# Down projection as a 2x2 block product with seven products, in a fused four-layer kernel on one Trainium2 core

## The reference

```python
gate = lora_add(einsum('bnh,fh->bnf', x, W_gate), x, A_gate, B_gate)
up   = lora_add(einsum('bnh,fh->bnf', x, W_up), x, A_up, B_up)
act  = silu(gate) * up                                   # F = 2752 features
down = lora_add(einsum('bnf,hf->bnh', act, W_down), act, A_down, B_down)   # H = 1024
x = x + down
```

## Time and profile before

| engine | busy us | share of the span | instructions |
|---|---|---|---|
| PE | 1717.8 | 96% | 8904 |
| PEld | 1472.5 | 82% | 8904 |
| DVE | 1136.5 | 63% | 1713 |
| ACT | 686.6 | 38% | 1095 |
| POOL | 341.7 | 19% | 407 |

### The profile page before, as it was taken

How to read it: one execution, slowest core, us unless ns; L and a number is a source line. 1 busy time by engine, 2 the same in 40 slices (tenths; PEclk the granted TensorE clock), 3 DMA queues, 4 the chain that set the end, 5 groups by cost and what they waited for, 6 DMA issues and landing times.

```text
span 1797.5 us, 28151 instructions
## 1 busy us (share of the span) xinstructions
PE 1717.8 (96%) x8904; PEld 1472.5 (82%) x8904; DVE 1136.5 (63%) x1713; ACT 686.6 (38%) x1095; POOL 341.7 (19%) x407
## 2 busy tenths in 40 slices
PE   6889999999998999998999999999989899989998
PEld 6778888888887887887888888888877777879997
DVE  4866667667754654335766666666658744348887
ACT  4333333333333442322333333333324322236655
POOL 5332222222220000001222222222210004002330
PEclk9899999999999999998999999999989999999999
DMA  8553323323334665534333233233235534466654
GB/s 253 186 137 106 103 93 105 105 94 108 107 118 152 210 215 192 189 135 160 101 104 102 95 106 103 93 104 106 76 111 187 175 109 153 158 242 236 241 181 188
DMA packets 100879, 258.00 MB, mean 144 GB/s; under 512 B 14818, under 2 KB 19074, under 8 KB 99810
## 3 DMA queue, kind: packets, MB, share of 16 engines
q1 hardware_dynamic: 73010, 186.70, 31.0%
q0 software_dynamic: 15728, 48.74, 8.7%
q10 hardware_dynamic: 12096, 22.03, 3.3%
HBM read 214.13 MB, written 49.58 MB: 147 GB/s over the span
## 4 chain that ended last, share of the span: by engine, by line
PE 80%; DVE 7%; issue 4%; SPq 3%; DMA 3%; ACT 2%; POOLq 1%; POOL 0%; another core or an unknown queue 0%; DVEq 0%; ACTq 0%
PE ps L1065 63%; PE ps L1319 5%; PE ps L1103 4%; PE ps L1316 3%; SPq L429 1%; DVE whl L1751 1%; DMA wraw<-in_wd 1%; PE ps L1348 1%; PE ps L1142 1%; PE ps L1144 1%; PE ps L1076 1%; ACT whl L736 1%; SPq L426 1%; PE ps L1332 1%; DVE act_hl L1755 1%
## 5 line engine op out<-in xcount | busy, mean ns | idle before, releaser
L1065 PE MATMUL ps<-act_hl,whl 128*128 128x512 f32 x2016 | 468.2, 394 | 14.2 <-DVE act_hl L1755 10.8
L1065 PE MATMUL ps<-xop,aop_a 128*128 128x512 f32 x2016 | 472.7, 390 | 0.0
L1065 PEld LDWEIGHTS ps<-act_hl,whl 128*128 128x128 f32 x2016 | 380.9, 190 | 99.7 <-DVE act_hl L1755 15.5
L1065 PEld LDWEIGHTS ps<-xop,aop_a 128*128 128x128 f32 x2016 | 372.9, 188 | 73.9
L1065 PE MATMUL ps<-xop,aop_b 128*128 128x512 f32 x1512 | 367.4, 392 | 6.7 <-DVE t L1714 6.3
L1065 PEld LDWEIGHTS ps<-xop,aop_b 128*128 128x128 f32 x1512 | 279.6, 189 | 62.2 <-DVE t L1714 4.9
L1751 DVE TENSOR_TENSOR whl<-wraw,whl 128x1024 fp32r<-128x1024 f32 x96 | 121.3, 1264 | 248.2 <-ACT whl L736 233.5
L736 ACT ACTIVATE whl<-wraw 128x1024 fp32r<-128x1024 f32 (+2 forms) x132 | 115.1, 888 | 355.9 <-PE ps L1065 297.3
L578 POOL DMA_INDIRECT lb_raw<-in_bgu,row_b x168 | 172.2, 1025 | 81.5 <-issue 38.4
L592 POOL TENSOR_SCALAR row_b<-row_b 128x4 int32<-128x4 int32 x40 | 24.0, 601 | 628.1 <-DVE lb_hl L1702 628.0
L1685 DVE TENSOR_TENSOR aop_b<-raw,aop_b 128x512 fp32r<-128x512 f32 x84 | 58.1, 692 | 107.8 <-ACT aop_b L736 107.7
(11 more groups left out here) (226 smaller groups left out, 2127.5 us busy)
## 6 DMA issues: line engine op xcount, KB each, us to landing
wraw<-in_wd SPq DMA_DIRECT2D x88, 512.0 KB
raw<-in_wgu SPq DMA_DIRECT2D x168, 256.0 KB, 3.1
rtoep<-k_dram SPq DMA_DIRECT2D x64, 512.0 KB, 4.3
act_raw<-act_dram SPq DMA_DIRECT2D x84, 256.0 KB
act_dram<-t ACTq DMA_DIRECT2D x42, 256.0 KB, 2.0
act_dram<-u ACTq DMA_DIRECT2D x42, 256.0 KB
xn<-in_x SPq DMA_DIRECT2D x16, 512.0 KB, 8.0
x0r<-x_dram POOLq DMA_DIRECT2D x16, 512.0 KB, 5.4
```

Of the source, the lines that this page charges most:

```text
L1065: ins = pe.matmul(bank, wt, r, start=start and k == 0 and n == 0, stop=stop and k == nk - 1 and n == 2, skip_group_check=True)
```

## The change

**The block product.** The first 20 feature tiles are two halves of ten (`NK = 10`), the 1024 outputs two halves of four banks. Halves of features, of outputs and the two chunks give a 2x2 block product, done with the same seven products as gate/up. Each product runs over ten tile pairs k. The 21st tile and the rest of 64 features (a "tail" step), and the LoRA product (an "adapt" step), are added as before, once for each of the four blocks of the result.

```diff
+def down_steps():
+    def tail(seg, block):
+        return [(seg, "tail", block, 0), (seg, "adapt", block, 0)]
+    def tiles(seg, i, ks):
+        return [(seg, "product", i, k) for k in ks]
+    return (tiles(0, Q1, range(NK)) + tiles(1, Q6, range(NK)) + tiles(2, Q2, range(NK)) + tail(2, (0, 0))
+            + tiles(3, Q5, range(NK)) + tiles(4, Q7, range(NK)) + tiles(6, Q3, range(NK // 2))
+            + tail(5, (1, 1)) + tiles(6, Q3, range(NK // 2, NK)) + tail(6, (0, 1))
+            + tiles(7, Q4, range(NK)) + tail(7, (1, 0)))
+GROUP = (0, 1, 0, 1, 0, 0, 1, 0)
+BANKS = ((6, 7, 0, 1), (2, 3, 4, 5))
+DIFFS = [i for i, d in enumerate(DOWN) if d[1] == "product" and d[2] in (Q6, Q7, Q4)]
+RAW_RING, HL_RING = 4, 3
```

```diff
+            def difference(p, s):
+                dve.wait_ge(draw_in[r], 32 * (total * p + m))
+                dve.wait_ge(y_in[n % 2], 16 * (len(DIFFS) // 2 * p + n // 2 + 1))
+                b = draw[r][:, 1, :]
+                tt(b, b, ysub[n % 2][:, :], ALU.subtract).then_inc(diff_done, 1)
...
+            def down(p, after):
+                for s in range(2, ND):
+                    if s + 1 in DIFFS:
+                        difference(p, s + 1)
+                    down_lo(p, s)
+                    for piece in after.get(s, ()):
+                        piece()
```

**In the frames.** DVE makes the other difference operand (activations of chunk 1 minus chunk 0) and it is stored too. In pass 0, frames 1 to 20 also make the four sums of weights that the products need, from a 512 KB load by SP, and POOL stores them (512 KB) to DRAM for both passes:

```diff
+            def weight_sums(v):
+                a11, a21, a12, a22, s1 = (wsum[:, i, :] for i in range(5))
+                dve.wait_ge(ws_in, 16 * (v + 1))
+                tt(s1, a21, a22, ALU.add).then_inc(ws_sum, 1)
+                dve.wait_ge(ws_sum, 4 * v + 1)
+                tt(a22, s1, a11, ALU.subtract).then_inc(ws_sum, 1)
+                tt(a21, a11, a21, ALU.subtract).then_inc(ws_sum, 1)
+                dve.wait_ge(ws_sum, 4 * v + 2)
+                tt(a12, a12, a22, ALU.subtract).then_inc(ws_sum, 1)
@@ DVE frame, after a_low of Q7 and Q2 and before the add of g1
+                if p == 0 and not (isinstance(f, int) and f == 0):
+                    weight_sums(f - 1)
@@ DVE frame, before the last act_low
+                if not last:
+                    tt(g0[:, :], t5[:, :], u3[:, :], ALU.subtract).then_inc(d_made, 1)
@@ POOL
             for f in range(1, NF):
                 load_lb(0, f)
+                pool.wait_ge(ws_sum, 4 * f)
+                pool.dma_start(ws_dram[f - 1], wsum[:, 1:5, :]).then_inc(ws_stored, 16)
@@ SP, end of the loads of frame f in pass 0
+                    reach(sp, ws_stored, 16 * (f - 1))
+                    sp.dma_start(wsum[:, 0:4, :].rearrange("p a w -> p (a w)"), wds[f - 1]).then_inc(ws_in, 16)
```

More of the change, by code:

```diff
@@ L432, in down_loads @@
[L432 to L464, removed]
@@ new lines, in down_loads @@
+            def down_loads(p):
+                for s in range(ND):
+                    load_down(p, s)
+                    if p and s == 50:
+                        sp.wait_ge(d_ev, n_evd(1, 4, 1))
+                        for i in range(4):
+                            sp.wait_ge(x1_stored[i], 16)
+                        sp.dma_start(x1s[:, 1, :, :], x1_dram[1]).then_inc(x1_in, 16)
+                if p:
+                    sp.wait_ge(k_stored, 32)
+                    sp.dma_start(x1s[:, 0, :, :], x1_dram[0]).then_inc(x1_in, 16)
@@ L790, in xraw_free @@
                 else:
-                    eng.wait_ge(x1_stored, 16 * 2)
+                    for i in range(4):
+                        eng.wait_ge(x1_stored[i], 16)
             def a_split(p, f, i):
@@ new lines, in frame, with down_hi @@
+                act_split(p, f, 1, 6, last)
+                act_split(p, f, 0, 8, last)
+                if not last:
+                    act.wait_ge(d_made, n_st(p, f) + 1)
+                    act.dma_start(act_dram[p, 2, f], g0[:, :]).then_inc(d_stored, 16)
+            def down_hi(p, s):
+                r = s % RAW_RING
+                kind = DOWN[s][1]
+                if kind == "adapt":
+                    act.wait_ge(bd_in, 32 * (4 * p + ADAPT.index(s) + 1))
+                else:
+                    n = sum(q % RAW_RING == r and q not in ADAPT for q in range(s + 1))
+                    total = sum(q % RAW_RING == r and q not in ADAPT for q in range(ND))
+                    act.wait_ge(draw_in[r], 32 * (total * p + n))
+                if s in DIFFS:
+                    act.wait_ge(diff_done, len(DIFFS) * p + DIFFS.index(s) + 1)
+                if s == 0:
+                    act.wait_ge(prod, n_f(p, NF - 1, PER_F) + USED_AT[Q7])
+                elif s == 1:
+                    act.wait_ge(prod, n_f(p, NF - 1, PER_F) + USED_AT[Q6])
+                elif s == 2:
+                    act.wait_ge(act_lo, n_act(p, NF))
+                else:
+                    act.wait_ge(*step_done(p, s - HL_RING))
+                copy(dhl[s % HL_RING][:, 0, :, :], draw[r][:, :, :]).then_inc(d_hi, 1)
@@ new lines, in save_p1, with form_last @@
+            def save_p1(p):
+                for half in range(2):
+                    act.wait_ge(d_done, bank_done(p, 0, 2 * half + 1))
+                    copy(p1_sb[p][:, 2 * half:2 * half + 2, :], banks_of(0, half)).then_inc(p1_saved, 1)
+            def down(p, after):
+                for s in range(2, ND):
+                    down_hi(p, s)
+                    for piece in after.get(s, ()):
+                        piece()
+            def form_last():
+                act.wait_ge(d_ev, n_evd(0, 4, 1))
+                form_hi(1, 6)
@@ new lines, in down_step @@
+            def down_step(p, s):
+                seg, kind, what, _ = DOWN[s]
+                hl = dhl[s % HL_RING]
+                begins = s == FIRST[seg]
+                start = begins and seg not in (2, 5, 6)
+                pe.wait_ge(d_lo, n_lo(p, s))
+                if kind == "adapt":
+                    pe.wait_ge(t_ready, p * 10 + 9 + what[1])
+                for j, b in enumerate(BANKS[GROUP[seg]]):
+                    if begins:
+                        free_banks(p, seg, j)
+                    cols = slice(j * P, j * P + P)
+                    bank = ps[:, b, :]
+                    if kind == "product":
+                        ins = split3(bank, lambda _: hl[:, 0, 0, cols], lambda _: hl[:, 1, 0, cols],
+                                     lambda _: hl[:, 0, 1, :], lambda _: hl[:, 1, 1, :], 1, start)
+                    elif kind == "tail":
+                        c = what[1]
+                        split3(bank, lambda _: hl[:, 0, 0, cols], lambda _: hl[:, 1, 0, cols],
+                               lambda _: act_hl[:, c, 0, :], lambda _: act_hl[:, c, 1, :], 1, False)
+                        for i in range(2):
+                            ins = pe.matmul(bank, hl[:, i, 1, cols], act_rest[:, c, :], start=False, stop=False,
+                                            skip_group_check=True)
+                    else:
+                        c = what[1]
+                        for half in range(2):
+                            for i in range(2):
+                                ins = pe.matmul(bank[:, half * HT:half * HT + HT], hl[:, i, half, cols],
+                                                t_hl[:, c, 0, half, :], start=False, stop=half == 1 and i == 1,
+                                                skip_group_check=True)
+                    if s == FINAL[seg]:
+                        ins.then_inc(d_done, 1)
+                if s != FINAL[seg]:
+                    ins.then_inc(d_used, 1)
@@ L1256, in _, with down @@
+            def down(p):
+                for s in range(ND):
+                    if p and s == 2:
+                        a_down(1, NF - 1)
+                    if p and s == FINAL[5] + 4:
+                        pe.wait_ge(d_ev, n_evd(1, 7, 1))
+                        s4d_kernel()
+                    down_step(p, s)
             for q in range(NQ):
@@ L1550, in kernel_rows @@
                 dve.wait_ge(kp, 1)
-                did(dve.tensor_copy(ksb[:, :, :].rearrange("p h j -> p (h j)"),
-                                    ps[0:LS, 0:4, :].rearrange("p a b -> p (a b)")))
+                for half in range(2):
+                    did(dve.tensor_copy(
+                        ksb[:, half * (C // 2):(half + 1) * (C // 2), :].rearrange("p (a h) j -> p a (h j)", a=2),
+                        banks_of(0, half)[0:LS, :, :]))
                 after()
@@ new lines, in difference @@
+            def difference(p, s):
+                n = DIFFS.index(s)
+                r = s % RAW_RING
+                m = sum(q % RAW_RING == r and q not in ADAPT for q in range(s + 1))
+                total = sum(q % RAW_RING == r and q not in ADAPT for q in range(ND))
+                dve.wait_ge(draw_in[r], 32 * (total * p + m))
+                dve.wait_ge(y_in[n % 2], 16 * (len(DIFFS) // 2 * p + n // 2 + 1))
+                b = draw[r][:, 1, :]
+                tt(b, b, ysub[n % 2][:, :], ALU.subtract).then_inc(diff_done, 1)
@@ L1832, in pass_, with down @@
+            def down(p, after):
+                for s in range(2, ND):
```

(10 more changed lines are left out.)

658 lines of the change are left out of this document (332 added, 326 removed).

## The result

The changed kernel took 1782.12 us in the median of four runs (1780.02 to 1782.82), the kernel before 1797.32 (1795.31 to 1799.87): a ratio of 0.9913, 95% interval 0.9896 to 0.993. That is 15 us faster where 68 were forecast: 37 us above the forecast's 1712 to 1745, and 14 us above the wider range that ends at 1768. The profiled execution spans 1780.7 us, 16.8 less than before.

What follows compares the result with a forecast made beforehand. PE was taken to bound the frames and pass 0's down stage, with DVE limiting part of pass 1's. Terms of -54.7, 0, -10, -4, -4, -7, +5 and +7 sum to -67.7 us: 1730 us forecast, range 1712 to 1745.

Steps and rivals of the forecast that it cites:

- Fewer matmuls: Tile steps: 240 fewer matmuls of 512 columns at 0.2278 us, -54.7 us if PE stays the bound.
- Splitting: Pass 0's down stage: DVE's splitting keeps up and PE stays the bound, 0 us, between -3 and +10.
- State-space kernel: Pass 1's down stage: losses of 20.4 us shrink to 10, so -10 us, between -17 and 0.
- The seams: Waits around the down stages shrink: pass 0's seam -4, between the passes -4, pass 1's restart -7 us.
- Frames of pass 0: Gathers behind the store of sums make a 22.2 us loop: +5 us over 20 frames, bounds 0 and +34.
- the sign that the prediction had set itself: The prediction is wrong if pass 0's frames are above 22.6 us.
- Rival B: Pass 0's frames: POOL's gather lands late, loop 23.7 us, +34 in place of +5, 1759 us; chance 0.12.
- Loads of the difference steps: Down stages: tiles for difference steps sometimes land late, +7 us, bounds 0 and +58.
- rival C: Down stages: difference-step loads land in 10 us, +94 in place of +7, 1817 us; chance 0.09.
- A: Only the matmuls go: no loss shrinks, frames cost 5 and steps 7 us, 1755 us; chance 0.17.
- A's 15: Sign for A: PE waits over 15 us on DVE's splits in steps 2 to 26 of pass 1.

Runs made afterwards that it cites:

- e5: e2 with pass 1's eight 512 KB residual loads moved from steps 6 to 9 to steps 24 to 27 of the down stage: 1723.7 us.
- e10: e2 plus the edits of e5 and e8, with the 2 MB x1 load cut into four at steps 50, 54, 58 and 62: 1712.59 us.
- e2: Changed kernel with POOL gathering the next frame's LoRA rows before each store of sums, and layer 0's weights before the last store: 1733.86 us.
- e8: e2 with SP asking for the raw tiles of steps 0 to 2 ahead of x for layer 0 in pass 0's seam: 1727.05 us.
- e6: Changed kernel with only the 512 KB load of the next weights moved from SP to POOL, behind the gathers: 1735.44 us.

## Why the prediction was wrong, by its own steps

1. *Fewer matmuls:* right. 1680 products and 96 of tails, 1776; in pass 0's stage 300 took 68.19 us, 0.2273 each:

```profile
715.05 68.19 PE L1150 MATMUL ps<-dhl 128*128 128x512 f32 x300
```

2. *Splitting:* right. Pass 0's stage 221.1 us (about 222 forecast), DVE 155 busy (161), PE idle for 3.2 us in all.

3. *State-space kernel:* right in sum, which is in part luck, as the parts were not. The stage with its restart gained 40.5 us; 27.35 + 10 + 7 less half of the 7 for loads are 40.9. But the largest waits in steps 2 to 26 were for third tiles behind the x0 loads (e5), which the prediction never counted as an event; only the 2 MB load of x1 was named, rightly (e10).

4. *The seams:* pass 1's restart went about as forecast (one wait of 1.35 us is left where 2 us of loss were), the units gained 1.6 of 4. Pass 0's seam lost 6.2 where 4 were to be gained. I had counted DVE's two splits (2.5 us) ahead of g1, but neither that POOL's eight gathers of layer 0's weights stand behind the last store (e2 removes that wait), nor that step 0's tile stands behind 4 MB of x on SP (e8; its expectation calls them 2 MB).

5. *Frames of pass 0:* this is the step that failed, +46 in place of +5, and with frames of 24.6 us the sign that the prediction had set itself (above 22.6) came true. The loop was the right one; the term that was wrong is the landing of the last gather, 7.7 us in the median in place of 4.9. Rival B, with a chance of 0.12, is what happened; its price was too low (+34), since the landing bound came from the start of the program. The loop was closed over POOL alone. SP, which waits for the same store and has the next frame's loads behind that wait, was left out of the step, though the wait stands in the diff. Costing bytes per frame (155 GB/s forecast, 158 in the window 349.47 to 373.52) hid that they come in one burst.

6. *Loads of the difference steps:* pass 0 lost at most PE's 3.2 us of waits to them, though DVE waited 20.0 us for third tiles there; in pass 1 they were late for a cause of its own (e5). That the sum of these stages came out so near is luck in part: pass 0's stage gained 3.9 us more than its share of items 1 and 6 (-27.35 + 3.5), the units 2.4 less. A loop like rival C did not form at 267 GB/s over the stage.

Rivals A and C are excluded by the stages: pass 1's gained 40.5 us where A leaves its stalls as they were, and PE's waits on DVE's splits in its first steps are 8.7 us in all, under A's 15; and pass 0's took 221 us, which leaves no room for C. Behind C stood an estimate worked out from a fit of the Trainium skill (DMA: Bandwidth & Descriptors, Anatomy of one DMA — SWDGE (gpsimd) path, not its section Bandwidth, as the prediction has it), 463 us for a pass's loads one after another. That fit is for DMAs issued from POOL, and these loads are issued from SP. The trace does not agree with the sum: the stage moved 267 GB/s at a DMA share of 0.80 in 221 us, so transfers of 256 KB overlap. The prediction's own row for this was misread: ahead of its window of 437 GB/s (1590 to 1595 us) SP issued two loads of 2 MB at 1587.47 and four of 512 KB behind them; the last of 256 KB went out at 1582.25.

## What to carry to other kernels

Where a change adds a wait to a queue, list what stands behind it there, DMAs above all: here one wait on SP for a reused tile turned four spread loads into a burst, on a loop with 0.3 us to spare. Here order mattered more than bytes: with the same transfers, putting four gathers ahead of one store gave back 48 us. And where a loop nearly fills a period, price it with the latency that the change itself will cause, or give the rival the larger chance.

## What was not expected of the hardware

A gather of LoRA rows behind a 512 KB store of the same POOL queue landed in 4.37 us (e6, 3.6 to 4.8 over its frames), as in 4.33 without one, so the store ahead of it cost nothing that shows here. Splitting that store made the program slower than before (1813 us). And a wait of PE cost more than its length: after 4.06 us of waiting in the changed kernel, 12 matmuls of 512 columns took 4.59 us where 3.0 are usual, at a mean granted clock of 0.63 over these 4.6 us, the 1.2 GHz level for part of them; the next 12, behind a wait of 0.65, had 1.00 again:

```profile
1381.00 4.59 PE L1150 MATMUL ps<-dhl 128*128 128x512 f32 x12 [4.06 <-DVE dhl L1910]
...
1386.24 3.03 PE L1150 MATMUL ps<-dhl 128*128 128x512 f32 x12 [0.65 <-DVE dhl L1910]
```
